# Four transformer-style sublayers on one core: weights packed on the host, transfers issued beside computing blocks, and a reordered local attention

## The reference, cut to what matters

```
x = LN(x + gated_delta(x))      # 16 heads, causal convolutions, recurrence
x = LN(x + ffn_L0(x))           # 2 layers of local attention + gated feed-forward
x = LN(x + wkv_mixer(x))        # low-rank mixes, 16 heads of size 8, recurrence
x = LN(x + ffn_L1(x))           # as ffn_L0, other weights

# one layer of ffn_L*: 8 heads of 64, windows of 64, keys of own and previous window
q, k, v = split(shift(x) @ wqkv)
q = rotate(q / max(norm(q), 1e-12) * q_scale);  k likewise
x = x + softmax(8 q k^T + mask) v @ wo
h = LN(shift(x)) * ln_g + ln_b
a, g = split(h @ w1 + b1);  x = x + (a * gelu(g)) @ w2 + b2
```

## Time and profile before

| | us |
|---|---|
| median of three runs (5920.3 to 5933.39) | 5931.38 |
| the profiled execution | 5919.51 |
| its span | 5917.7 |
| one attention layer, first `hT` to last `residual` | about 351 (four of them) |
| one feed-forward | about 99 to 101 (four of them) |
| one norm | about 28 to 30 (four of them) |

### The profile page before, as it was taken

The page is one execution under the profiler, slowest core; times in us unless marked ns, Lnnn a source line. Parts: engine busy times, 40 slices in busy tenths (PEclk is TensorE's granted clock), DMA queues, the critical chain, the costliest instruction groups (busy, mean ns, idle before and its releaser), DMA issues. The chain is left out here.

```text
span 5917.7 us, 106596 instructions
## 1 busy us (share of the span) xinstructions
PE 5154.2 (87%) x36898; PEld 3594.3 (61%) x36898; DVE 3964.4 (67%) x8910; ACT 2823.5 (48%) x6606; POOL 2226.4 (38%) x1555
## 2 busy tenths in 40 slices
PE   5999999999899999999969889884488786988998
PEld 3677677776676776776746546541156664654665
DVE  5655656656556656556569759836699546975994
ACT  1444444444444444444448748834400114874883
POOL 2433424424334334334246426514422113652661
PEclk8999999999999999999989989986699657998998
DMA  2000000000000000000000000000000000000000
GB/s 108 6 5 7 5 5 7 5 5 7 5 7 6 4 7 5 5 7 5 6 27 0 22 4 0 0 5 0 8 1 1 1 0 27 0 23 4 0 0 14
DMA packets 181393, 53.02 MB, mean 9 GB/s; under 512 B 151876, under 2 KB 177432, under 8 KB 180376
## 3 DMA queue, kind: packets, MB, share of 16 engines
q1 hardware_dynamic: 179880, 49.26, 3.7%
q10 hardware_dynamic: 1392, 2.20, 0.1%
HBM read 40.93 MB, written 10.49 MB: 9 GB/s over the span
## 5 line engine op out<-in xcount | busy, mean ns | idle before, releaser
L342 PE MATMUL gd_ps<-gd_taps,gd_xwin 128*128 128x512 f32 x2048 | 906.4, 598 | 8.0 <-ACT gd_qT L528 8.0
L342 PEld LDWEIGHTS gd_ps<-gd_taps,gd_xwin 128*128 128x128 f32 x2048 | 382.3, 190 | 465.0 <-issue 445.5
L787 POOL TENSOR_TENSOR gd_o_rn<-gd_tmp,gd_mhalf 128x8 f32<-128x8 f32 x64 | 103.6, 1637 | 1192.2 <-DVE gd_tmp L706 1192.2
L551 ACT ACTIVATE gd_X<-gd_ps 128x512 f32<-128x512 f32 x512 | 268.3, 633 | 540.0 <-PE gd_ps L384 539.9
L683 DVE TENSOR_TENSOR gd_Z<-gd_ps,cst 128x256 f32<-128x256 f32 x384 | 163.0, 424 | 326.0 <-PE gd_ps L422 259.9
L781 POOL TENSOR_TENSOR gd_gate<-gd_gate,gd_norm_w 128x2048 f32<-128x2048 f32 x32 | 145.1, 4536 | 480.0 <-ACT gd_gate L516 480.0
L384 PE MATMUL gd_ps<-cst,gd_gV 128*128 128x128 f32 x2048 | 263.7, 277 | 54.7 <-DMA gd_gV<-gd_inverses 31.4
L384 PEld LDWEIGHTS gd_ps<-cst,gd_gV 128*128 128x128 f32 x2048 | 225.2, 143 | 77.9 <-ACT gd_decay L546 75.1
L516 ACT ACTIVATE gd_v<-gd_ps 128x512 f32<-128x512 f32 x128 | 76.4, 597 | 406.2 <-PE gd_ps L342 406.2
L431 PE MATMUL gd_ps<-gd_Z,gd_X 128*128 128x64 f32 x2048 | 239.2, 275 | 0.0
L422 PE MATMUL gd_ps<-gd_gV,gd_nA 128*128 128x64 f32 x2048 | 236.0, 273 | 0.0
(11 more groups left out here) (441 smaller groups left out, 14017.9 us busy)
## 6 DMA issues: line engine op xcount, KB each, us to landing
L_ffn_sb_rope<-in_rope SPq DMA_DIRECT2D x4, 2048.0 KB, 8.2
gd_tap_row<-in_L_attn_conv_v SPq DMA_DIRECT2D x2, 2048.0 KB, 7.2
gd_blocks<-gd_nA SPq DMA_DIRECT2D x256, 16.0 KB, 1.7
gd_Z<-gd_blocks SPq DMA_DIRECT2D x32, 128.0 KB, 2.0
gd_inverses<-gd_Z SPq DMA_DIRECT2D x32, 128.0 KB, 1.7
gd_gV<-gd_inverses SPq DMA_DIRECT2D x256, 16.0 KB, 1.9
L_ffn_sb_wqkv<-in_L_ffn_wqkv SPq DMA_DIRECT2D x4, 768.0 KB, 8.3
gd_tap_row<-in_L_attn_conv_q SPq DMA_DIRECT2D x1, 2048.0 KB, 15.2
```

What stands on the lines that cost most here:

```text
L342: ins = pe.matmul(ps[4 + i % 2][:], xwin[:, t:t + P] if i < 8 else xwin[:, PAD:PAD + P], taps[:, t, 512 * SLICE[i]:512 * (SLICE[i] + 1)] i ...
L551: act.activation(heads(X, gi).rearrange("p h x -> p (h x)"), ps[4 + gi][:], ACT.Copy).then_inc(x_s.sem, 1)
```

## The change

Host side: `ffn_vectors`, `ffn_second`, `ffn_scales` and `wkv_weights` pack the small inputs, the last one with the transposes done on the host, so that a feed-forward's parameters come in 3 transfers instead of 13, an attention's in 4 instead of 9, and all of `wkv_mixer`'s in 1 instead of 30.

Blocks: a class `Beside` gives the computing blocks extra work for each engine. The loads of layer 0, the primes, the masks, the memsets (now once per `ffn_block`, on POOL) and the first `rope` multiplication stand inside the norm's block; `load_attention(1)` and the second `rope` multiplication stand inside the first feed-forward, `load_feed_forward(1)` inside the second attention, the mixer's transfer inside norm n2. The feed-forward's loops are written out.

Attention: `rotate_*` waits for the projection and `squares_*` for the rotation; the floor is a `tensor_reduce` with max over pairs (sum, 1e-24) in a new tile `sf`; the order in the steps of PE, ACT and DVE is another one, and `residual`, `keep_k` and `scale_o` stand one step elsewhere relative to the tile.

```diff
+        def load_feed_forward(sp, layer):
             sp.dma_start(w1[:], W["w1"][layer]).then_inc(la.f_loaded, 16)
-            for k, (lo, hi) in enumerate(HID_CUTS):
-                sp.dma_start(w2[0:hi - lo, k], W["w2"][layer, lo:hi]).then_inc(la.f_loaded, 16)
...
+            sp.dma_start(w2[:], W["second"][layer]).then_inc(la.f_loaded, 16)
+            sp.dma_start(vecs[:], W["vectors"][layer]).then_inc(la.f_loaded, 16)
+
+        def scale_rotations(dve, layer):
+            dve.wait_ge(la.loaded, (layer + 1) * (16 * 2))
+            dve.tensor_tensor(rope[:], rope[:], scales[:].unsqueeze(1).to_broadcast([P, NC, 4, AD]), ALU.mult)
+
+        class BesideNorm(Beside):
+            def sync(self, sp):
                 load_attention(sp, 0)
                 sp.dma_start(masks[:, 0:2], A["masks"]).then_inc(la.f_const, 16)
                 load_feed_forward(sp, 0)
...
+            def pool(self, pool):
+                tiles.set_constants(pool)
+                tiles.clear_halos(pool)
+                pool.wait_ge(la.f_const, 16)
+                pool.tensor_copy(masks[:, 2:NC], masks[:, 1:2].to_broadcast([P, NC - 2, P]))
...
+            def vector_late(self, dve):
+                scale_rotations(dve, 0)
+
+        class BesideAttention(Beside):
+            def sync(self, sp):
+                load_feed_forward(sp, 1)
+
+        class BesideFeedForward(Beside):
+            def sync(self, sp):
+                load_attention(sp, 1)
...
+            def vector_late(self, dve):
+                scale_rotations(dve, 1)
+
+        post_norm(nc, cst, [norm_of], norm_of, sems, norm_tag, xo, pads, BesideNorm())
...
+        attention_layer(nc, cst, xo, xa, la, tiles, masks, rope, wqkv, wo, ps, 0, Beside())
+        feed_forward(nc, cst, xa, xo, la, w1, w2, vecs, L, 0, f"{pre}0", BesideFeedForward())
+        attention_layer(nc, cst, xo, xa, la, tiles, masks, rope, wqkv, wo, ps, 1, BesideAttention())
+        feed_forward(nc, cst, xa, xo, la, w1, w2, vecs, L, 1, f"{pre}1", Beside())
...
+            def squares_k(b, c):
...
+                w(la.rot_k.now(tile(b, c)))
+                act.activation(sq[b][:, K], ps_k[:], ACT.Square).then_inc(la.sq_k.sem, 1)
...
             def norm_k(b, c):
...
-                    dve.scalar_tensor_tensor(sk, sk, 1e-24, sk, ALU.max, ALU.max).then_inc(la.ss_k.sem, 1)
+                dve.tensor_reduce(ss[b][:, AH:2 * AH], sk, AX_X, ALU.max).then_inc(la.ss_k.sem, 1)
...
+                    if c == 1:
+                        beside.vector_late(dve)
...
+                beside.vector_late(dve)
```

More of the change, by code:

```diff
@@ L899, in ffn_block, with tensor, scalar, vector @@
+class Beside:
+    def sync(self, sp):
+        pass
+    def tensor(self, pe):
+        pass
+    def scalar(self, act):
+        pass
+    def pool(self, pool):
+        pass
+    def vector(self, dve):
+        pass
+    def vector_late(self, dve):
+        pass
+def ffn_block(nc, A, cst, pre, xo, xa, sems, norm_of, norm_tag, pads):
     la = LocalAttention(nc, sems)
-    W = {n: A[pre + n] for n in ("wqkv", "q_scale", "k_scale", "wo", "ln_g", "ln_b", "w1", "b1", "w2", "b2")}
+    W = {n: A[pre + n] for n in ("wqkv", "scales", "wo", "w1", "second", "vectors")}
@@ L1380, with feed_forward @@
 FW = 512
[L1383 removed]
+def feed_forward(nc, cst, xin, xout, la, w1, w2, vecs, L, layer, pre, beside):
+    turn0 = layer * (T // FW)
     with ExitStack() as ctx:
@@ L1401, in _ @@
                 w = lambda x: pool.wait_ge(*x)
-                with pool.Fori(0, T // FW) as c:
+                pool.memset(mhalf[:], -0.5).then_inc(la.f_half, 1)
+                beside.pool(pool)
+                pool.wait_ge(la.f_half, layer + 1)
+                for c in range(T // FW):
                     n = turn0 + c
@@ L1410, in _ @@
                 w = lambda x: pe.wait_ge(*x)
-                with pe.Fori(0, T // FW) as c:
+                pe.wait_ge(la.f_loaded, (layer + 1) * (16 * 3))
+                for c in range(T // FW):
                     n = turn0 + c
@@ L1443, in _ @@
                 w = lambda x: act.wait_ge(*x)
-                with act.Fori(0, T // FW) as c:
+                act.wait_ge(la.f_loaded, (layer + 1) * (16 * 3))
+                for c in range(T // FW):
                     n = turn0 + c
@@ L1460, in _ @@
                 w = lambda x: dve.wait_ge(*x)
-                with dve.Fori(0, T // FW) as c:
+                dve.wait_ge(la.f_loaded, (layer + 1) * (16 * 3))
+                for c in range(T // FW):
                     n = turn0 + c
@@ L1499, in post_norm, with _ @@
         with nc.Block() as block:
+            @block.sync
+            def _(sp):
+                beside.sync(sp)
             @block.tensor
             def _(pe):
+                beside.tensor(pe)
                 for i in range(n):
```

882 lines of the change are left out of this document (433 added, 449 removed).

## The result

| | before | after |
|---|---|---|
| median, us | 5932.4 (5920.3 to 5942.4, 4 runs) | 5771.0 (5767.6 to 5775.1, 4 runs) |
| the profiled execution | 5919.5 | 5775.1 |
| ratio of the medians | | 0.9734, 95% interval 0.9722 to 0.9746 |

The change takes 161 us off the median, where 130 were forecast (5932 to 5802). The profiled execution before was the quickest of its runs and the one after the slowest of its own, so the two traces show only 144.4 us of it.

The account below looks back on a forecast made before the run. Attention was taken as bound by DVE and an equally long chain of waits (10.30 us a step); 83.8 us from joints plus 40 from attention off 5919.5 gave 5795.5, plus 6 about 5802; forecast 5780 to 5822, 52%.

Parts of the forecast that it names:

- the joints: Stretches between blocks where nothing computes: loads and set-up move under neighbouring blocks, norm cost included, 83.8 us gained.
- norms longer: Norms n1 and n3: table multiplication and mask copy beside the norm delay its powers, 1.5 us each, -3.
- attention to feed-forward, first layers: Pause of 8.51 us: SP's nine issues go under the feed-forward, 2.0 stay; gain 6.5, twice, 13.0.
- feed-forward to attention, less the multiplication: Pause of 8.82 us shrinks to 0.5, DVE's table multiplication is paid in full at 4.42; gain 3.9, twice, 7.8.
- The ring: Attention step: waits from one `project_k` to the next without slack, 10.30 us before, 9.98 after the change.
- the mis-sized tail of PE: End of the attention step: behind `turn_q`, 0.6 plus 1.0 us for `output` before `project_k`, setting the step at 9.98.
- The rival of the shorter ring: Attention: `turn_q` 0.15 to 0.3 us earlier, first steps gain too; step 9.7, 74 us for four layers, 5768; 16%.
- The first steps: Start of each attention layer: left unchanged in the sum, as was the drain; no gain counted.
- Both limits have to move.: Attention step: DVE's work and the chain of waits both last 10.30 us; unless both shrink, the step stays.
- the rival in which the port goes to POOL: Attention: `keep_v` waits for POOL's addition; step 10.84 to 11.0, 67 to 87 us lost, 5909 to 5928; 10%.
- an addition above 1.27: Attention on POOL: an addition longer than 1.27 us in the profile after would show a port conflict and a wrong forecast.
- the rival "the loads don't hide": Masks hold each norm by 10 us, the multiplication costs PE's clock in two feed-forwards; 20 to 25 back, 5825; 10%.

Follow-up runs that it names:

- the first tail experiment: ACT's `copy_v_shifted` moved behind `copy_q` of the next step, against the changed kernel: 5749.4 us, ratio 0.97, step 9.68 us.

## Why the prediction was right, and where it was not

The side was right and 5771 lies in the range of 5760 to 5860, but below the forecast's own 5780 to 5822. The difference of 31 us has four parts: the attention gained 66 instead of 40 us, the joints 85 instead of 84, other stretches lost 6.5 in the traces (5.5 of it before the change begins: `gated_delta` ends at 2964.65 instead of 2959.18), and 10 are the offset between profiled run and median, where I added 6 and the run after lay 4 above its median. 26 + 1.5 - 6.5 + 10 = 31.

| term, us | forecast | traces |
|---|---|---|
| ahead of n1 and n3 | 31.0 | 15.5 + 14.7 |
| norm to attention, twice | 18.0 | 9.2 + 9.2 |
| norms longer | -3 | -4.8 - 0.7 |
| attention to feed-forward, first layers | 13.0 | 8.15 + 8.1 |
| the same, second layers | 0.8 | 2.2 + 2.3 |
| feed-forward to attention, less the multiplication | 7.8 | 8.5 - 5.5 + 8.1 - 5.7 |
| mixer | 16.2 | 15.9 |
| attention, four layers | 40 | 15.1 + 18.0 + 15.9 + 16.9 |

- **The ring.** From the power on its working held to a hundredth up to `turn_q` (8.40); ahead of the power errors cancelled. The step that failed is the last one, the mis-sized tail of PE: 0.6 + 1.0 = 1.6. It is 1.46 in the changed kernel, where `hT` is ready only 0.14 us ahead of the next `project_k` (3115.53, 3115.67), and 0.49 + 0.89 = 1.38 in the first tail experiment, where PE's queue alone decides. The forecast put PE's end (9.98) behind ACT's (9.86). The ACT end was right to the hundredth and is the one that decides; PE's is 9.68, as that experiment shows. 0.12 x 124 = 15 us. The rival of the shorter ring named 5768, near the result, but by a step of 9.7, which is not what happened.
- **The first steps "left as they are".** That was the other error. Of the 66 us, 0.44 x 124 = 55 are the step as forecast and result read it, 10.30 and 9.86, in one place. Over all steps the means are 10.31 and 9.84, which is some 4 us more. The remaining 7 to 8 lie in the first four steps of each layer. In the second attention these took 45.0 us before (3488.46 to 3533.47) and 40.6 after (3447.76 to 3488.34), 4.4 less where four steps at the steady rate give 1.9. The rows of the first 30 us, before and then after:

```profile
3487.78:3517.78 30.00, 19.69 (x96) 9.16 (x96) 18.45 (x36) 11.79 (x23) 16.54 (x12) 0.67 0.00 1
```

```profile
3447.04:3477.04 30.00, 20.47 (x136) 10.23 (x138) 17.46 (x41) 14.98 (x31) 18.55 (x14) 0.77 0.07 19
```

  PE comes in from a pause of 0.3 instead of 8.8 us and gets a clock of 0.77 instead of 0.67. But the pause is the smaller part: the kernel with the joints alone has the short pause and the old steps, and there these four steps take 44.0 us (at a clock of 0.72), 1.0 less than before. The rest came only with the attention's own edits. The shorter-ring rival had named a gain of the first steps, by the pause; the sum had not taken it in.
- **"Both limits have to move."** No run bears this out. The ring was there, and its new order alone, with the old floors, brought the step to 9.91. DVE was busy without a bracket, but it did not hold the ring up: in the kernel with the floor alone it waits 0.62 us and the rotation is no earlier. What that kernel gained, 0.15, is the floor as the last wait of the ring. Nor was DVE's time the two floors' fixed 1.82 us. The order alone moves it, since it changes when the floor meets POOL. The prediction quotes the rule for that (whoever starts first keeps the port) and prices the floors as constants all the same. The time did not suffer, as the floor was part of the change anyway.
- **`keep_v` and the port.** Right: 0.42 stays, the addition takes 1.51 instead of 1.27, and the rival in which the port goes to POOL did not come. By the Trainium skill ("SBUF — State Buffer", section Who interferes with whom) a copy in a two-port mode and a GpSimd instruction exclude each other, and the first one holds on. The trace agrees that the second one is held up, 1.51 us with the copy beside it and 1.28 without; it is about 0.24 us longer, though 0.37 of the copy lay beside it. The prediction had allowed for the addition's wait (end at 4.17, measured 4.23), but its list of signs called an addition above 1.27 a sign of being wrong: the sign came and the forecast did not fail by it. For in this order the 0.24 us were on no path that decides.
- **The norm.** The mechanism was not the one I priced. In n1 POOL's copy of the masks started at 2983.65 within the multiplication (2982.24 to 2986.66) and took 4.54 instead of 1.68 us, the powers began 18.0 us after the norm's start, yet PE went from column sums to spreading without a pause:

```profile
2981.43 11.15 PE L1579 MATMUL n_ps<-cst,n_sq 128*128 128x1 f32 x64
...
2983.65 4.54 POOL L1017 COPY L_ffn_sb_masks<-L_ffn_sb_masks 128x1792 f32<-128x1792 f32 x1 [11.07 <-DMA L_ffn_sb_masks<-in_masks]
...
2988.15 7.83 POOL L1608 TENSOR_TENSOR n_rstd<-n_var,n_mhalf 128x4 f32<-128x4 f32 x8
...
2992.43 9.95 PE L1584 MATMUL n_ps<-cst,n_rstd 128*128 128x128 f32 x64
```

  The cover held. The 4.8 us go with PE's clock, 0.69 against 0.79. The same norm took 28.74 us at 0.80 in the kernel with `keep_v` early, and 32.59 at 0.70 in the kernel with the floor alone, which has nothing beside its norm. The rows of the kernel before and of that one:

```profile
2980.24:3009.05 28.81, 26.94 (x144) 21.53 (x144) 15.05 (x32) 10.09 (x16) 8.01 (x11) 0.79 0.02 2
```

```profile
2983.42:3016.01 32.59, 30.72 (x144) 25.00 (x144) 15.04 (x32) 10.08 (x16) 8.12 (x11) 0.70 0.01 2
```

  So the term is nearer to 0.5 (n3's 28.98 against 28.29) than to 1.5, and n1's length in one trace says nothing on the change.
- **Joints.** Attention to feed-forward left 0.36 instead of 2.0. The table load of 1.28 us that I let stay is gone from there, and with it what the second layers still waited for (2.61 to 0.37). The feed-forward's ACT instructions fell from 55 to 49 and their time from 40.53 to 32.45 us, 6 x 1.28 and some; the table loads inside it went from seven to one. The kernel with the joints alone has 0.36, 0.37 and once 0.67 there, so it belongs to the joints: the written-out loop or the missing block, which no run separates. Feed-forward to attention was 8.5 instead of 8.3, but the multiplication cost 5.5 to 5.7 against the feed-forward before, where 4.42 were counted: it costs its own time and then a low clock behind it. That half of the rival "the loads don't hide" came, and with it a sign of being wrong: PE stood idle for 4.72 us, ahead of 3398.24, where 4.4 were allowed.

## What to carry to other kernels

Where several waits end together, list every path to the same instruction with its length to a tenth: here ACT's tail and PE's tail were 0.18 us apart, two edits that gave -22 and +10 us alone gave -76 together, and an edit that removed a true conflict of 0.24 us gave nothing, and later cost 28, though the same conflict cost about 0.1 us a step where the addition came last. Work that is moved beside other work should be cut into pieces that fit the engine's idle gaps: 16 pieces of 0.41 us were free, one of 4.42 cost 7. And an instruction's long time in a profile may be a wait for another engine's instruction, so it goes with the order, not with the instruction.
